# End of attention: copies of probabilities ahead of weight splits on ScalarE, a new order of VectorE's steps, expert weights loaded in halves

## The reference

```python
B, Sq, _ = x.shape                       # 16, 256, 256
q, k, v = heads(layernorm(x) @ w_q), heads(context @ w_k), heads(context @ w_v)
attn = softmax(einsum('bhid,bhjd->bhij', q, k) * SCALE, axis=-1)
x = x + merge(einsum('bhij,bhjd->bhid', attn, v)) @ w_o + b_o
x_flat = layernorm(x).reshape(N, D)
gates = softmax(x_flat @ router_w + router_b)          # 8 experts, top 2 of them
pos = cumsum(expert_mask, axis=0) - 1                  # place in the expert, at most 640
h = gelu(einsum('ecd,edh->ech', buf, w1) + b1[:, None, :])
out = einsum('ech,ehd->ecd', h, w2) + b2[:, None, :]
y = einsum('ned,ne->nd', out[e_idx, pos_g], gates * valid)
return x + y
```

## Time and profile before

| | |
|---|---|
| median of three runs | 913.05 us (910.46 to 913.29) |
| the profiled execution | 914.2 us |
| its span, first to last instruction | 912.4 us |
| PE busy | 882.8 us (97%) |
| DVE busy | 727.7 us (80%) |
| ACT busy | 535.9 us (59%) |
| POOL busy | 403.2 us (44%) |
| mean granted clock of TensorE | 0.990 of 2.4 GHz |

### The profile page before, as it was taken

One profiled execution on the slowest core, in us unless ns is written; L12 is line 12 of the kernel. 1 busy time (PEld: TensorE's weight loads), 2 busy tenths in 40 slices (PEclk: granted clock), 3 DMA queues, 4 the chain that ended last, 5 costly groups with the idle time before them and its releaser, 6 DMA issues.

```text
span 912.4 us, 21639 instructions
## 1 busy us (share of the span) xinstructions
PE 882.8 (97%) x7552; PEld 781.9 (86%) x7552; DVE 727.7 (80%) x1580; ACT 535.9 (59%) x1535; POOL 403.2 (44%) x622
## 2 busy tenths in 40 slices
PE   7999999999999999999999999997899999999995
PEld 7877888888888888888888888886799999999995
DVE  5776789898988989898998988986877787668762
ACT  5875676676766676676676766765443354334520
POOL 5553435545464554646545465433333222332223
PEclk9999999999999999999999999999999999999998
DMA  8577888888888878888788888777239556554322
GB/s 234 154 224 242 257 239 257 235 251 239 259 250 245 262 218 258 253 246 269 220 244 254 237 244 251 227 213 223 82 112 198 101 100 146 132 134 64 97 29 29
DMA packets 154427, 180.94 MB, mean 198 GB/s; under 512 B 62300, under 2 KB 127946, under 8 KB 150480
## 3 DMA queue, kind: packets, MB, share of 16 engines
q1 hardware_dynamic: 128784, 143.97, 53.6%
q10 hardware_dynamic: 16704, 26.62, 11.2%
q0 software_dynamic: 8832, 8.98, 5.8%
HBM read 106.00 MB, written 78.47 MB: 202 GB/s over the span
## 4 chain that ended last, share of the span: by engine, by line
PE 72%; DVE 10%; DMA 8%; ACT 5%; issue 2%; SPq 1%; ACTq 0%; POOLq 0%; POOL 0%; DVEq 0%
PE psum L814 21%; PE psum L1082 10%; PE psum L1066 10%; PE psum L925 10%; PE psum L881 8%; PE psum L941 8%; DMA squares<-prob 4%; ACT prob L1154 3%; DVE hidl L1302 2%; DVE prob L1385 2%; DMA inverses<-invturned 1%; PE psum L904 1%; DVE bufl L1302 1%; DMA invrows<-inverses 1%; DMA probt<-squares 1%
## 5 line engine op out<-in xcount | busy, mean ns | idle before, releaser
L1154 ACT ACTIVATE prob<-psum,negmax 128x256 f32<-128x256 f32 x512 | 239.2, 485 | 122.5 <-DVE negmax L1356 105.4
L1356 DVE TENSOR_REDUCE negmax<-psum 128x2 f32<-128x512 f32 x256 | 158.4, 681 | 35.6 <-PE psum L881 35.4
L684 POOL TENSOR_TENSOR al<-attended,ah 128x512 fp32r<-128x512 f32 x57 | 73.7, 1292 | 193.8 <-ACT ah L1093 193.7
L790 POOL DMA_INDIRECT out_rows<-y,rowi x40 | 66.3, 1658 | 159.0 <-DVE y L1614 135.6
L1385 DVE STREAM_TRANSPOSE prob<-prob 128x1024 f32<-128x1024 f32 x116 | 127.5, 1099 | 6.1 <-ACT prob L1154 5.9
L925 PE MATMUL psum<-probt,v 128*64 128x256 f32 x1024 | 126.0, 389 | 1.9 <-DMA probt<-squares 1.9
L1274 ACT ACTIVATE hid<-psum,b1t 128x640 f32<-128x640 f32 x64 | 50.9, 796 | 126.6 <-PE psum L1066 126.6
L1154 ACT ACTIVATION_READ_ACCUMULATOR prob<-psum,negmax 128x1 f32 x512 | 111.0, 217 | 0.0
L925 PEld LDWEIGHTS psum<-probt,v 128*64 128x64 f32 x1024 | 68.5, 137 | 39.6 <-issue 7.3
L1082 PE MATMUL psum<-w2h,hidh 128*128 128x256 f32 x320 | 91.2, 285 | 1.4 <-DVE hidl L1302 1.4
L1082 PE MATMUL psum<-w2l,hidh 128*128 128x256 f32 x320 | 90.5, 283 | 0.0
(11 more groups left out here) (212 smaller groups left out, 2602.8 us busy)
## 6 DMA issues: line engine op xcount, KB each, us to landing
squares<-prob SPq DMA_DIRECT2D x29, 1024.0 KB, 4.8
squares<-prob SPq DMA_DIRECT2D x29, 768.0 KB, 6.2
invrows<-inverses SPq DMA_DIRECT2D x128, 128.0 KB, 4.0
probt<-squares SPq DMA_DIRECT2D x58, 256.0 KB, 5.0
probt<-squares ACTq DMA_DIRECT2D x58, 256.0 KB, 5.8
probt<-squares SPq DMA_DIRECT2D x58, 192.0 KB, 3.8
probt<-squares ACTq DMA_DIRECT2D x58, 192.0 KB, 4.4
w1r<-in_w SPq DMA_DIRECT2D x8, 1024.0 KB, 5.2
```

Source lines behind the costliest of these rows:

```text
L684: pool.tensor_tensor(al[:, b % 2, c:c + 2, :], attended[:, :, :], ah[:, b % 2, c:c + 2, :].bitcast(F32), ALU.subtract).then_inc(sem("a_lo" ...
L790: pool.indirect_dma_start(out=out_rows, out_offset=bass.IndirectOffsetOnAxis(ap=rowi[:, e % 2, s:s + 1], axis=0), in_=y[:, e % 2, s, :], i ...
L1154: last = act.activation(into, out_of, ACT.Exp, bias=negmax[:, m % 2, u, qb:qb + 1], accum_out=total[:, m % 2, u, qb:qb + 1])
L1356: dve.tensor_reduce(negmax[:, m % 2, u, :], psum[:, u, :].rearrange("p (q s) -> p q s", q=ST), AX.X, ALU.max, negate=True).then_inc(sem("m ...
```

## The change

Nothing is computed otherwise. ScalarE takes `copy0` of 62 ahead of `w_hi` 0, and the four pieces of weights each one or more steps later than before. VectorE takes `inv` 63 ahead of `w_rest` 0, `x2add` 29 and what follows it between pieces, `pick` 13 behind `a_norm` 62, `ln2` 14 behind `a_lo` 62, `row_lo` 14 behind `a_norm` 63, `shift` 14 behind `center`, and `w_rest` 3 behind `pick` 14, the last step ahead of the experts. SP loads w1 of an expert e of 1 or more as soon as the first two pieces of the expert before are split, and w2 as before when all four are. TensorE's `o_most` 31 has five chunks in place of six, and `o` 31 three in place of two.

```diff
@@ -202,21 +202,20 @@
-            *steps("exp0 exp1", z), ("w_hi", 0), ("a_hi", m - 1), ("copy0", m), *steps("exp2 exp3", z), ("w_hi", 1),
-            *steps("copy1 copy2 copy3", m), ("gate_exp", c), ("v_sb", z), ("w_hi", 2), *steps("copy0 copy1", z),
-            ("w_hi", 3), ("a_hi", m), *steps("copy2 copy3", z), ("x2t_sb", d), ("row_hi", d), ("a_hi", z),
+            *steps("exp0 exp1", z), ("copy0", m), ("a_hi", m - 1), *steps("exp2 exp3", z), ("copy1", m), ("w_hi", 0),
+            *steps("copy2 copy3", m), ("gate_exp", c), ("v_sb", z), ("w_hi", 1), *steps("copy0 copy1", z),
+            ("w_hi", 2), ("a_hi", m), *steps("copy2 copy3", z), ("x2t_sb", d), ("row_hi", d), ("a_hi", z), ("w_hi", 3),
             ("gate_exp", d), ("x2t_part_sb", o0), ("x2t_part_sb", o1), ("scale", e), ("row_hi", e), ("gate_exp", e),
             ("gelu_table", 0)]
...
-            *steps("compare rank", c), ("w_rest", 0), ("w_rest", 1), ("x2add", ST * d + 1), ("ln2_stats", d), *steps("slot gate", c), ("inv", z),
-            *steps("keys pick", c), ("a_norm", m), ("ln2", d), ("a_lo", m), ("w_rest", 2), ("w_rest", 3),
-            ("row_lo", d), ("a_norm", z), *steps("bias compare", d), ("a_lo", z), *steps("rank shift", d),
-            ("x2add", o0), ("stat", o0),
-            ("x2add", o1), ("stat", o1), ("center", o0), ("center", o1), *steps("slot high onehot carry", d),
-            *steps("bias compare rank", e), *steps("gate keys", d), *steps("row_lo slot high onehot shift", e),
-            ("pick", d)]
+            *steps("compare rank", c), ("inv", z), ("w_rest", 0), ("x2add", ST * d + 1), ("ln2_stats", d),
+            *steps("slot gate keys", c), ("a_norm", m), ("pick", c), ("a_lo", m), ("ln2", d), ("w_rest", 1),
+            ("w_rest", 2), ("a_norm", z), ("row_lo", d), *steps("bias compare", d), ("a_lo", z), ("rank", d),
+            ("x2add", o0), ("stat", o0), ("x2add", o1), ("stat", o1), ("center", o0), ("center", o1), ("shift", d),
+            *steps("slot high onehot carry", d), *steps("bias compare rank", e), *steps("gate keys", d),
+            *steps("row_lo slot high onehot shift", e), ("pick", d), ("w_rest", 3)]
@@ -555,9 +554,12 @@
                 if e >= 1:
+                    sp.wait_ge(sem("wsplit_hi"), WSPLITS * e - WSPLITS // 2)
+                    sp.wait_ge(sem("wsplit_lo"), WSPLITS * e - WSPLITS // 2)
+                sp.dma_start(w1r[:, :, :], w1[e].rearrange("(k p) n -> p k n", p=P)).then_inc(sem("w1_in"), 16)
+                if e >= 1:
                     sp.wait_ge(sem("wsplit_hi"), WSPLITS * e)
                     sp.wait_ge(sem("wsplit_lo"), WSPLITS * e)
-                sp.dma_start(w1r[:, :, :], w1[e].rearrange("(k p) n -> p k n", p=P)).then_inc(sem("w1_in"), 16)
                 sp.dma_start(w2r[:, :, :], w2[e].rearrange("(k p) n -> p k n", p=P)).then_inc(sem("w2_in"), 16)
@@ -943,11 +945,15 @@
+            def most(n):
+
+                return PAIRS - 2 - n % ST
+
             def o_most(n):
-                o(n, range(PAIRS - 2))
+                o(n, range(most(n)))
 
             def o_(n):
-                o(n, range(PAIRS - 2, PAIRS) if n >= ST * (B - 1) else range(PAIRS))
+                o(n, range(most(n), PAIRS) if n >= ST * (B - 1) else range(PAIRS))
```

## The result

The changed kernel has a median of 906.92 us over five runs (906.53 to 907.06), the kernel before in the same comparison 913.05 (910.46 to 913.62, five runs): a ratio of 0.9927, with an interval of 0.9907 to 0.9948. By the medians it is 6.1 us faster. The forecast was 906.8, from 903.5 to 911.0.

A forecast was written before the change was run, and what follows sets the result against it. TensorE's own work was taken as the bound, with gains only from its idle time and slow clock. spread0 moving from 661.2 to 654.9 saves 6.3 us: 913.05 less 6.3 gives 906.8, range 903.5 to 911.0.

The forecast's parts named there:

- The hole at `turn3`, 5.24 us, and its clock, 2.03: PE idle 5.24 us from 632.10, then 4.06 us at half clock, worth 2.03; both were to go.
- The copies behind `w_hi` 0: copy2 and copy3 of 62 on ScalarE still wait for w_hi 0, leaving PE 0.7 us idle at turn0 of 63.
- `a_norm` 62, set by `inv_in` 62: VectorE's step starts at 640.9, after inv_in 62 lands at 640.8; PE waits 0.8 us and resumes at 643.4.
- The inverses of 63: On SP, inv_out 63 takes 2.0 us, inv_in 63 lands at 644.1, needed at 646.6; taking 7.3 would cost 2.8.
- rival 2: inv_in 63 arrives late and the wait moves to the inverses; saving 3.5 us, time 909.6 us, chance 0.10.
- The chain behind it: VectorE's chain after PE resumes: a_lo 63 at 648.7, x2t_part at 652.8, spread0 at 654.9 instead of 661.2.
- Three matmuls out of `o_most` 31 and weights in halves, 0: Matmuls removed from o_most 31 are worth 0, hidden by VectorE's chain; earlier w1r for experts 2 to 7 also 0.
- `w_rest` 3 in an idle stretch, 0: Its 1.27 us on VectorE ahead of the experts fits an idle 1.85 us: costs 0, or 1.27 without that gap.
- Its effect on w2r of expert 1, 0 with 14 us to spare: On SP, w2r of expert 1 goes out near 663.4, lands near 672.5, is wanted at 687.0; 14 us remain.
- Rival 1: Clock stays up in the spreads (4.10 us at 0.58 before); another 1.5 us gained, 905.3 us, chance 0.15.
- Rival 3: VectorE is the bound all along, other waits refill its 4.83 and 1.91 us holes but for 2; 911 us, chance 0.11.
- Rival 4: Small PE gaps between 636.6 and 654.9 drop the clock to 0.50; 6.7 us slower, 919.8 us, chance 0.06.

The follow-up runs named there:

- e4_fill: The kernel before with 40 needless transposes on TensorE filling the idle time ahead of turn3 of 62; median 911.75 us, ratio 0.9982.
- e3_nohalf: Changed kernel with w1 and w2 loads again waiting for all four pieces and o_most 31 in six chunks; median 908.12 us, ratio 0.9940.
- f2_rest3: Changed kernel with w_rest 3 back ahead of a_norm 63 and w_hi 3 ahead of a_hi 62; median 910.14 us, ratio 0.9956.
- g4_order: g3_pool without GpSimd's pieces: w_rest 2 last on VectorE ahead of the experts, w_rest 3 behind expert 0's third tile; median 918.34 us, ratio 1.0013.
- f1_again: The changed kernel as it is, run once more in another comparison against the kernel before; median 908.35 us, ratio 0.9925.
- e1_act: The kernel before with ScalarE's new order alone, w_hi 3 staying ahead of a_hi 62; median 910.38 us, ratio 0.9974.
- f3_control: The changed kernel as it is, run again as control beside h1_one and g3_pool; median 913.83 us, ratio 0.9976.
- h1_one: e1_act with one more move, w_rest 1 from behind w_rest 0 to behind a_lo 62 on VectorE; median 913.77 us, ratio 0.9978.
- g3_pool: Changed kernel with w_rest 2 and 3 moved to GpSimd, SP's order of g2_sp, and pieces 0 and 1 later; median 918.20 us, ratio 1.0019.
- g2_sp: Changed kernel with SP issuing inv_out 62 ahead of w1r, w2r behind inv_in 62; row_lo 14 ahead of a_norm 63, w_hi 2 later; 910.27 us, ratio 0.9954.

## Why the prediction was right, point by point

The mechanism came out as forecast, wait by wait, and the points below show it. That the median lies within 0.2 us of the number is luck in part: the sum leaves out the clock of the spreads, which gave 0.8 us more in the profiled execution, the profile that it was worked out in lay 1.15 above its median, and the same kernel gained 5.2 and 3.1 us in two other comparisons.

- **The hole at `turn3`, 5.24 us, and its clock, 2.03**: right. After has neither, and e4_fill prices the clock at 1.84.
- **The copies behind `w_hi` 0**: a gap of 0.7 was taken for `turn0` of 63 and 0.23 measured. w1r was taken to be there 6.4 us after its issue, as before; `w_hi` 0 started 5.86 after it, with no wait (it landed after 5.6). It changed nothing in the sum, since the next wait took it up.
- **`a_norm` 62, set by `inv_in` 62**: taken for 640.9, at 640.85, behind 1.09 idle. SP's issue stood at 637.26 before and 637.30 after, as said. The wait at `o_most` 30 is 1.19 in place of 0.8, since PE came sooner and resumed at 643.21 (643.4 taken).
- **The inverses of 63**: 2.0 was taken for the way of `inv_out` 63 and 2.3 measured (638.59 to 640.85), so rival 2 did not happen: `a_norm` 63 waited 0.28, and for PE.
- **The chain behind it**: `a_lo` 63 at 648.51 (648.7), `x2t_part` at 652.75 (652.8), `spread0` at 654.72 (654.9). The sum of 6.3 measures 6.48, or 6.14 with `x2t` 13 as zero in both.
- **Three matmuls out of `o_most` 31 and weights in halves, 0**: e3_nohalf shows no difference.
- **`w_rest` 3 in an idle stretch, 0**: right. The gap of 1.85 before `bufl` has shrunk to 0.30 (after) behind it, so it is just covered. What it would cost without cover was put at 1.27; f2_rest3 measured 0.95 in its old place.
- **Its effect on w2r of expert 1, 0 with 14 us to spare**: it went out at 662.82 (663.4 taken) and delayed nothing. g4_order shows that the spare time is shorter than the 14 us worked out from ACT's want of w2r: some 10 us later the load meets scatters, `rows` and `b_all`, and the experts lose up to 3.8.
- **Rival 1, the clock**: it came true in the profiled execution and not in f1_again. 1.5 was put on it; the spreads differ by 1.0 (6.64 less 5.63) between two profiles of this kernel. It was set apart as a case of the kernel; the runs show that it is one of the execution. Of six executions of f1_again the fastest, 906.14 us, had a mean clock of 0.997, the slowest, 912.21, one of 0.993.
- **Rival 3, DVE is the bound**: half right. After the change it is the bound from 641 to 654 (f2_rest3), but its holes did go. With ScalarE's order alone it takes most of the gain back (e1_act).
- **Rival 4, slower by the clock**: after had 1.00 through all its small gaps. But in e1_act a gap of 3.62 was enough for 0.51, and in f1_again the clock fell right behind 1.32 and 0.56. The prediction said that the gap of 1.60 "left the clock at 1.00"; its own rows show that only up to the spreads, and 0.58 from 661.20 on the earlier trace rows.

What the prediction had not: that the gain differs between comparisons, 6.1, 5.2 and 3.1 us, the last with the late releases of f3_control.

## What to carry to other kernels

A copy or split that waits for a large load belongs behind everything on its engine that needs no such data; look for a timeline row with a long DMA wait, and for who stands behind it. Then walk the next engine with the new times before the change is made: ScalarE's order alone gave 2.2 us, VectorE's alone nothing, both 4.5 in the same comparison and 6.1 in another, because each saving ran into the other's queue. When work is moved to a less busy engine or a later place, count the ports that it shares and all that is queued behind its semaphore.

## What the runs showed of the hardware

- **The clock falls in one execution and not in another of the same kernel.** Three of 14 profiles have the spreads in under 6 us, the others in 6.6 or more, and one kernel is in both groups (5.63 and 6.64). The Trainium skill (TensorE: Matmul & The Clock Gate, What's actually happening) says that the monitor that sets the clock runs free of the kernel's start; the traces agree, as far as one kernel with both outcomes can show it. Longer gaps go both ways too: behind 2.71, 2.85 and 2.94 us of idle at `turn3` of 62 (h1_one, f3_control, g3_pool) the clock stayed at 1.00, behind 2.78 (g4_order) it was 0.50 at once. The same four transposes take 0.65 us in f3_control and 1.07 in g4_order:

```profile
637.85 1.07 PE L910 MATMUL psum<-ident,prob 128*128 128x128 f32 x4 [2.78 <-ACT probt L1103]
```

A difference of 1 us in one pair of profiles says nothing of a change here.
- **GpSimd blocks VectorE**: 128x64 instructions of 0.21 us took 1.89 and 2.39 beside GpSimd's 128x1024 subtractions of 2.5 us (g3_pool), and at most 0.23 without them (g4_order).
- **A small DMA behind a large one**: `inv_out` 62, behind 2 MB on SP's queue, let `inv_in` be issued 7.5 us later (629.79 to 637.30); `inv_out` 63, alone, 2.3. Put ahead of the weights (g2_sp), `inv_out` 62 took 2.8.
- **Late releases**: in four of 14 profiles engines that waited for PE went on 2.2 to 3.7 us after the recorded end of its work, and two engines that waited for different results did so within 0.1 us of each other. The DMA share is high there (0.86 to 1.11 from 633 to 639 in f3_control), but as high at the same place in after, which has no such wait. What does it stays open; that the matmuls' recorded ends are modelled leaves room for PE itself having been late. No run here tells the two apart.
